# Delta-rule attention: chunks of 8 tokens solved in two halves of 4, with masked key products that carry the errors on

## What is computed

```
def step(S, t):
    q_t, k_t, v_t, a_t, b_t = t
    y = einsum('bhvk,bhk->bhv', S, k_t)
    err = y - v_t
    S = a_t[..., None] * S - (b_t[..., None] * err)[..., None] * k_t[:, :, None, :]
    o = einsum('bhvk,bhk->bhv', S, q_t)
    return (S, o)
```

## Time and profile before

| | us |
|---|---|
| median of 3 runs | 2726.8 |
| traced execution | 2720.65 |
| its span | 2718.9 |
| delta attention, its setup to its last block | about 986 to 2400 of the span |
| one part of 32 tokens, from the first base to the first state addition | 78.8 |

### The profile page before, as it was taken

How to read it: one execution, slowest core, us unless ns; L and a number is a source line. 1 busy time by engine, 2 the same in 40 slices (tenths; PEclk the granted TensorE clock), 3 DMA queues, 4 the chain that set the end, 5 groups by cost and what they waited for, 6 DMA issues and landing times. The chain is left out here.

```text
span 2718.9 us, 42746 instructions
## 1 busy us (share of the span) xinstructions
PE 2081.5 (77%) x15844; PEld 1636.3 (60%) x15856; DVE 1592.5 (59%) x3191; ACT 1141.1 (42%) x2723; POOL 1175.9 (43%) x996
## 2 busy tenths in 40 slices
PE   7597449978988968657896578955689656768798
PEld 5364126656566857646776567755568655546586
DVE  2223732246664339668776787766778677546533
ACT  3112311136464428434464344743446434325433
POOL 0222022210004535968339683386733877300254
PEclk9698769979998979767797677976779757789899
DMA  8422022210007023422223222232222332020340
GB/s 282 125 24 53 0 69 43 24 38 2 22 2 231 0 34 109 126 95 94 86 74 125 96 94 86 74 119 101 94 77 80 111 114 93 32 56 2 93 138 15
DMA packets 137426, 212.96 MB, mean 78 GB/s; under 512 B 61184, under 2 KB 113680, under 8 KB 132112
## 3 DMA queue, kind: packets, MB, share of 16 engines
q1 hardware_dynamic: 129072, 200.11, 23.1%
q0 software_dynamic: 8160, 10.26, 2.4%
HBM read 187.97 MB, written 22.37 MB: 77 GB/s over the span
## 5 line engine op out<-in xcount | busy, mean ns | idle before, releaser
L2088 PE MATMUL PS<-ident,XT 128*128 128x128 f32 x512 | 112.8, 402 | 258.2 <-DVE XT L2460 245.5
L2402 DVE SCALAR_TENSOR_TENSOR XT<-M_delta,CW_delta,XT 128x256 f32<-128x256 f32 x576 | 249.9, 495 | 70.2 <-ACT M_delta L2271 40.6
L2088 PEld LDWEIGHTS PS<-ident,XT 128*128 128x128 f32 x512 | 90.4, 208 | 277.6 <-DVE XT L2460 132.7
L2037 PE MATMUL PS<-XP_delta,X 128*128 128x268 f32 (+1 forms) x1024 | 241.6, 388 | 5.5 <-DMA X<-in_L_attn_b_heads 5.5
L2037 PEld LDWEIGHTS PS<-XP_delta,X 128*128 128x128 f32 x1024 | 192.7, 189 | 55.7 <-issue 11.4
L1541 PE MATMUL PS<-XP_rffn,UW_rffn 128*128 128x512 f32 x816 | 194.6, 395 | 5.5 <-POOL UW_rffn L1495 4.6
L1976 POOL TENSOR_TENSOR DD_delta<-DD_delta,A_delta 128x64 f32<-128x64 f32 (+6 forms) x224 | 169.9, 759 | 39.2 <-ACT A_delta L2359 19.5
L1541 PEld LDWEIGHTS PS<-XP_rffn,UW_rffn 128*128 128x128 f32 x816 | 155.5, 191 | 39.5 <-issue 6.8
L1273 ACT ACTIVATE PR_attn<-PS,NM_attn 128x256 f32<-128x256 f32 (+1 forms) x384 | 130.7, 448 | 103.6 <-DVE NM_attn L1343 103.6
L1495 POOL TENSOR_TENSOR UW_rffn<-W_rffn,UW_rffn 128x512 fp32r<-128x512 f32 x34 | 44.1, 1298 | 296.0 <-ACT UW_rffn L1602 296.0
L561 POOL DMA_INDIRECT sums<-XS_moe,token_moe x46 | 71.7, 1559 | 221.0 <-ACT XS_moe L661 205.8
(11 more groups left out here) (414 smaller groups left out, 5068.6 us busy)
## 6 DMA issues: line engine op xcount, KB each, us to landing
M_delta<-gram_delta SPq DMA_DIRECT2D x32, 2304.0 KB, 8.7
X<-in_L_attn_b_heads SPq DMA_DIRECT2D x64, 512.0 KB, 3.4
EW<-in_L_ffn_w SPq DMA_DIRECT2D x24, 512.0 KB, 10.0
CB_rffn<-routes_rffn SPq DMA_DIRECT2D x20, 512.0 KB, 22.4
XN<-in_L_attn_b_outs SPq DMA_DIRECT2D x16, 512.0 KB, 3.6
F_delta<-in_L_attn_b_outs SPq DMA_DIRECT2D x4, 2048.0 KB, 8.5
W_rffn<-in_L_ffn_tiles SPq DMA_DIRECT2D x4, 1536.0 KB, 11.6
slots<-pad SPq DMA_DIRECT2D x2, 2967.0 KB, 14.7
```

The source lines that it names most:

```text
L2037: last = nc.tensor.matmul(PS[:, 1 + i, 0:B * (WIN - halo)], WH[:, r, i, k, :], XP[:, k, :, n * BT + halo:n * BT + WIN], start=(k == 0), st ...
L2088: last = nc.tensor.transpose(PS[:, 6 + r % 2, i * P:(i + 1) * P], W[:, B * h:B * (h + 1), :], core.ident[:])
L2402: nc.vector.scalar_tensor_tensor(TMP[:, r, i], RAW[:, r, i, :, tau:tau + BT], CW[:, i, h, tau:tau + 1], TMP[:, r, i], ALU.mult, ALU.add).t ...
```

## The change

- A chunk is solved in two halves of 4 tokens (`HC`). The pairs kept in `M` and `DD` fall from 36 to 20 per lane, all within a half. `solve` runs three pairs of instructions per half.
- What the first half's errors do to the second half is made by TensorE: VectorE writes the errors times decays (`WH4`, `wh_d`), TensorE transposes them (2 transposes, `ht_mm`), ScalarE copies them (`NH4`, `nh_d`), TensorE multiplies them with `GH` (8 products, `res_mm`), and VectorE applies decays (`carry`) and adds.
- `GH` and `GN` are masked key products, made once per part (`key_products`): 32 and 96 products of separately copied keys (`keys_apart`), copied out by ScalarE and multiplied on GpSimd by beta and a mask that keeps a lane's own rows (`own_lanes`). For that, beta is also computed in rows in the stage's setup, turned, and moved through DRAM (`BETAC`, `BETAH`).
- What earlier chunks do to the next one is made by hops: 4 transposes of one chunk's `WNS`, one copy on ScalarE, 16 products with `GN` (`hop`). Chunk `jj` has `jj + 1` hops. The sum is accumulated in PSUM over a part of zeros (`ZB`).
- `W` is turned for the state update only once per part of 32 tokens; its first three chunks are copied there by ScalarE (12 copies).
- ScalarE's lanes per chunk are 10, 18, 18, 18. `DC` has two buffers. The answer copy comes after the next step in ScalarE's order (`answer`). The small tiles of `Norm` become slices of one scratch tile, the same size of work everywhere.

The core of the diff. GpSimd's products of decays, in `prepare`:

```diff
-                for t in range(C - 1, 0, -1):
-                    last = nc.gpsimd.tensor_tensor(DD[:, :, tri(t - 1) + 1:tri(t)], DD[:, :, tri(t):tri(t + 1)],
-                                                   step(t).broadcast_to([P, BH, C - t]), ALU.mult)
-                    if t > 1:
+                for u in range(HC - 1, 0, -1):
+                    last = nc.gpsimd.tensor_tensor(dd[:, :, :, tri(u - 1) + 1:tri(u)], dd[:, :, :, tri(u):tri(u + 1)],
+                                                   av[:, :, :, u:u + 1].broadcast_to([P, BH, 2, HC - u]), ALU.mult)
+                    if u > 1:
...
+                c.then(nc.gpsimd.tensor_tensor(dr[:, :, 1:], dd[:, :, 1, 0:HC], av[:, :, 1, 0:1].broadcast_to([P, BH, HC]), ALU.mult))
+                c.then(nc.gpsimd.tensor_tensor(dc[:, :, 1:HC + 1], dd[:, :, 0, 0:HC], av[:, :, 0, 0:1].broadcast_to([P, BH, HC]), ALU.mult))
+                c.then(nc.gpsimd.tensor_tensor(dc[:, :, HC + 1:], dr[:, :, 1:], dc[:, :, HC:HC + 1].broadcast_to([P, BH, HC]), ALU.mult))
```

TensorE, the order within a chunk, and a hop:

```diff
+                        first_half(n, ci)
+                        if jj == 0:
...
+                        elif jj < NI - 1:
+                            pe.wait_ge(res_d, z["res_d"] + ci + 1)
+                            for k in range(4):
+                                nc.tensor.matmul(PS[:, 1 + k, 0:4 * QU], ZB[:, 0:P], ZB[:], start=True, stop=False)
+                            for x in range(jj):
+                                hop(n, o, jj, x)
                         pe.wait_ge(w_d, z["w_d"] + ci + 1)
-                        if jj:
+                        if jj + 1 < NI:
+                            hop(n, o, jj, jj)
+                        else:
                             pe.wait_ge(wdec_d, z["wdec_d"] + rests(o, jj))
-                        for r in range(NR):
-                            turn(n, ci, r)
-                        if jj + 1 < NI:
-                            rest(n, o, jj + 1)
+                            for r in range(NR):
+                                turn(n, o, r)
...
+            def hop(n, o, jj, s):
...
+                if s < jj:
+                    pe.wait_ge(wdec_d, z["wdec_d"] + rests(o, jj))
+                for i in range(4):
+                    last = nc.tensor.transpose(PS[:, 6, i * P:(i + 1) * P], WNS[:, s, i * P:(i + 1) * P], core.ident[:])
+                last.then_inc(nw_mm, 1)
...
+                pe.wait_ge(nw_d, x)
+                for i in range(4):
+                    for k in range(4):
+                        rows, at = slice(OC * k, OC * (k + 1)), slice(i * QU, (i + 1) * QU)
+                        last = nc.tensor.matmul(PS[:, 1 + k, at], NEW[rows, i], GN[rows, BLOCKS.index((s, jj + 1)), at], start=jj == 0,
+                                                stop=jj == 0 or (s == jj and i == 3))
+                if s == jj:
+                    last.then_inc(rest_mm, 1)
```

ScalarE, the order within a chunk:

```diff
+                        if jj == NI - 1:
+                            act.wait_ge(wdec_d, z["wdec_d"] + rests(o, jj - 1))
+                            for x in range(NI - 1):
+                                for i in range(4):
+                                    last = nc.scalar.copy(W[:, :, x * C:(x + 1) * C].rearrange("p (k i b) t -> p i k b t", i=4, b=B)[:, i],
+                                                          WNS[:, x, i * P:(i + 1) * P].rearrange("p (k b t) -> p k b t", k=4, b=B))
+                            last.then_inc(nat_d, 1)
+                        act.wait_ge(ht_mm, z["ht_mm"] + ci + 1)
+                        nc.scalar.copy(NH4, PS[:, 7, 0:BH * HC]).then_inc(nh_d, 1)
...
+                        elif jj < NI - 1:
+                            for x in range(jj):
+                                hop(n, o, jj, x)
                         for lane in range(cuts[jj], cuts[jj + 1]):
                             last = nc.scalar.activation(S[:, lane, :], S[:, lane, :], ACT.Copy, scale=AO[:, lane:lane + 1])
-                        if jj == NI - 1:
+                        if jj < NI - 1:
+                            hop(n, o, jj, jj)
+                        else:
```

VectorE, `chunk`, between the two halves and behind the second:

```diff
+                solve(k, 0)
                 dve.wait_ge(ds_d, z["ds_d"] + o + 1)
...
+                base(o, jj, r, 1, FQ).then_inc(base_d, 1)
+                dve.wait_ge(wh_d, z["wh_d"] + ci + 1)
+                c.then(nc.vector.tensor_tensor(near, near, HJ[:, :, jj, 1:2].broadcast_to([P, BH, HC]), ALU.mult))
+                dve.wait_ge(res_mm, z["res_mm"] + ci + 1)
+                c.then(carry(r, 0))
+                c.then(nc.vector.tensor_tensor(FK[:, :, HC:], FK[:, :, HC:], carried(0), ALU.add))
+                solve(k, 1)
...
+                carry(r, 1).then_inc(res_d, 1)
```

416 lines of the change are left out of this document (302 added, 114 removed).

## The result

The changed kernel takes 2789.4 us (median of four runs, 2784.8 to 2790.6), the kernel before on the same chip 2725.0 (2723.1 to 2727.4): a ratio of 1.0233, 95% interval 1.0215 to 1.0251, or +64 us where +81 was forecast. (A block is 340 to 343 us long before, by its first bases at 1114.9, 1454.9, 1798.1 and 2141.3, and not about 320.) The page gives the span and busy times of the changed kernel; in the earlier trace rows GpSimd was busy for 1175.9 us, VectorE for 1592.5.

A forecast was written before the change was run, and what follows sets the result against it. GpSimd was taken to bound the chunks, VectorE 1.2 us behind. 4 x (3.7 + 11.2) + 16 + 5 = 81 us on 2720.65 gave 2801.7, and 2808 us with the median 6.2 higher; range 2725 to 2855.

The forecast's parts named there:

- GpSimd no longer bounds: Inner chunks: GpSimd drops from 21 to some 15.5 us and no longer bounds.
- The decay chain: A part's decay chain on GpSimd: four strided products of 512, up to 2.25 us each, 9 us, as much as before.
- W to late product: Behind `w_d`: late product after 11.25 us (second chunk), 14.9 (third), against VectorE's 6.9; stalls 4.3 and 8.0 us.
- First parts +3.7: Each block's first part of four chunks: 82.5 us against 78.8, +3.7.
- Second parts +11.2: Each block's second part, with gates on TensorE: 93.3 us at low clock, 80 at full, taken at 90, +11.2.
- Setup +16: Stage setup: beta in rows, turned and moved by DMA, all behind the old end: +16 us, between 10 and 22.
- States +5: States: seven more ScalarE copies, 1.2 us per block where no gap is: +5 us (0 to 10).
- A (clock): Rival: PE at full clock in the parts, shrinking hops, round trips and gates: +18, 2745 us; chance 0.16.
- B (VectorE ends each chunk): Rival: second and third chunks, late product within 6.9 us of `w_d`: faster, -41, 2686 us; chance 0.15.
- C (GpSimd dearer): Rival: GpSimd's three- and four-dimensional instructions cost 40% more than by elements: +48, 2856 us; chance 0.07.

The follow-up runs named there:

- its order mended: Changed kernel with GpSimd's decays within the next chunk issued ahead of its own lanes on the later key products: 2793.8 us, ratio 1.0256.
- The lanes alone: Changed kernel with ScalarE's state lanes behind the copy of the chunk's last hop instead of ahead of it: 2752.5 us, ratio 1.0119.
- The split: Changed kernel with the last third of the later key products behind the first half in a part's first chunk: 2806.6 us, ratio 1.0307.
- lanes and carries moved: Changed kernel with ScalarE's lanes behind the hop's copy and both VectorE carries ahead of the second half's solve: 2716.0 us, ratio 0.9984.

## Why the prediction was right, and which terms were off

*GpSimd no longer bounds.* Right. Its parts went from 75.0 busy us to 64.5, and inside a first part only the second chunk's base waits for it (2.4 us; 1.1 in three of four with its order mended). From one query product to the next (1508.74 to 1523.71) it needs 15.0 us in an inner chunk, 15.5 forecast. The forecast's own terms do not give its "5.7 us less", though: seven products of decays summed to 5.3 us before, so 3.0 + 2.25 less, and 1.0 more for the start decays, make 4.2. GpSimd also loses less to VectorE's key product now, but no run separates that.

*The decay chain.* The row's stride price held and not the rule of the Trainium skill cited there: the forecast had up to 2.25 us for each of four products, the trace has 2.1 to 2.2 (two of the first three, and the fourth):

```profile
1470.06 4.31 POOL L2018 TENSOR_TENSOR X<-X,A_delta 128x512 f32<-128x512 f32 x2
1474.44 2.11 POOL L2019 TENSOR_TENSOR HJ_delta<-X,A_delta 128x512 f32<-128x512 f32 x1
```

*W to late product.* Right in place, chain and length. From the base to the end of W 10.35 us were forecast, 10.4 measured (with a round trip twice as long the forecast's terms give 12.65, not its 12). From base to base 21.6 and 25.25 us were forecast, 21.4 and 25.2 measured. The stall in the third chunk came as forecast (8.15 for 8.0), that in the second at half (2.2 for 4.3), because one term of VectorE's own work was undersized: the key product took 3.60 us, not 1.6, in that place. The sum did not notice, since the stall only shrank by as much. That the chain is what costs is shown by the two edits that shorten it: together they take back .0249 of the time, all of the .0233 lost, although the setup's 15 us remain. The lanes alone, of which the forecast says "nothing hides them", were under half of it (.0114 of the .0249): 3.1 of their 5.35 us ran beside a hop's products and transposes on TensorE. The forecast's sum already has them so, beside the first hop; only its sentence does not.

*First parts +3.7.* Measured +5.1: the last chunk 16.1 to 16.5 instead of 15.65, and the first 19.5 to 22.1 instead of 20, with TensorE's key products issued in pieces with gaps of 1.3 and 2.0 us. The split shows that VectorE's wait there is not what costs; what sets the second base is GpSimd's order behind these products.

*Second parts +11.2.* Measured +11.1, and that is in part luck. The forecast's chunks (22, 23.6, 27.3, 20.4) sum to 93.3 at the low clock, and it took 90 for a clock in between without saying where that helps. Measured are 24.0, 22.2, 26.85 and 17.5: the first is 2 us too short in the forecast, the last 3 us too long. There the granted clock was 0.75, the four gates took 4.8 us and not 5.9, and the twelve copies behind them 0.21 us each and not 0.28.

*Setup +16.* From the end of beta (1012.9) to the first head weight pass 15.7 us, before 0.7: +15.0, of the forecast's 15.6. The products take 6.2 (4.9 forecast) and start 1.0 ahead of beta's end; sigmoids 1.3, turn 1.1, write 2.2, six issues 3.5 (2.4 forecast), landing 2.3.

*States +5.* Wrong, and the one term with the wrong sign: the forecast had ScalarE's seven copies lengthen the states, and the stretches between parts came out 10 us shorter. The heads' stretches took 141.1, 146.2 and 143.4 us before and 140.2, 140.2 and 140.9 after; in the other twelve profiled executions, all with the changed states, they take 139.3 to 142.0. So the copies' 1.2 us a block do not show, and two stretches of the one execution before were long. In the 146.2 the last of 128 small products was issued 4.4 us late:

```profile
1792.78 0.24 PE L2046 MATMUL PS<-KQ_delta 128*32 128x64 f32 x1 [4.38 <-issue]
```

In the 143.4 the granted clock was 0.92 where the 141.1 had 0.95, and TensorE was busy for 132.4 us in place of 129.4. Both look like chance of that execution; no second profile of the kernel before is there to show it.

*The rivals.* A (clock): the parts were granted 0.54 to 0.55 and 0.66, close to the 0.52 and 0.66 that the forecast took. With the waits shorter and the same products it is a little higher: 0.55 to 0.58 and 0.72 with lanes and carries moved. B (VectorE ends each chunk) needed the late product within 6.9 us of W; it took 10.8. With lanes and carries moved, B's mechanism came true at the third chunk's base, which no longer waits, but after 19.1 us and not 17.3, with a key product of 3.7 in them; the last chunk's base still waits 2.9 in first parts. C (GpSimd dearer): its packed products cost what elements said (1280 elements 2.9 us).

## What to carry to other kernels

When a result starts to travel through a second and third engine before its owner may go on, list what each of these engines has queued in front of it: here the small scalings on ScalarE held nobody up in the kernel before, where the bases waited for GpSimd, and 18 of them stood in the chain after. Release the far part of such a chain as early as its data are there, before the owner's own next work. And take a wait away only where the next wait is not for somebody else: removing the longest one of a first chunk made the kernel slower, because GpSimd was later than it.

## What the hardware showed

- **VectorE's product of two SBUF tiles and a GpSimd product exclude each other.** The key product (1264 elements) takes 1.47 or 1.48 us when GpSimd is idle at its start. At 1524.37 it finds GpSimd in its query product and ends at 1527.97, 1.33 us after GpSimd ended at 1526.64 (first line; the second is a key product with GpSimd idle):

```profile
1523.71 2.93 POOL L2092 TENSOR_TENSOR M_delta<-M_delta,DD_delta 128x1280 f32<-128x1280 f32 x1
...
1545.77 1.48 DVE L2658 TENSOR_TENSOR M_delta<-M_delta,DD_delta 128x1264 f32<-128x1264 f32 x1
```

  At 1484.32 it is the same: GpSimd's subtraction ends at 1485.50, the key product 1.34 us later. All 17 of the 32 key products that start while GpSimd works end 1.33 or 1.34 us after that GpSimd instruction; the other 15 take 1.47 or 1.48. The key product waits whole, it does not slow down. The Trainium skill says so too (SBUF — State Buffer, Who interferes with whom: an exclusive lock on the port pair shared by the two); the trace agrees.
- **GpSimd over a stride of four costs 4.1 ns an element**, 2.11 us for 512 with a result and both operands strided, against 2.1 to 2.5 ns packed (1.05 to 1.28 us for 512).
- **Small matmuls are issued in pieces.** The 192 matmul records of the later key products, 16 ns apart where they flow, come with gaps for which nothing in the profile is to blame:

```profile
1487.33 2.04 PE L2215 MATMUL PS<-KQ_delta,XT 128*32 128x64 f32 x128 [1.34 <-issue]
1491.36 1.17 PE L2215 MATMUL PS<-KQ_delta,XT 128*32 128x64 f32 x38 [2.00 <-issue]
```

  Their places vary from block to block.
- **The same code takes up to 10 us more where the granted clock is lower.** Turns, update and states of the second half take 42.8 us at 0.76 in the second block (the row of 1571.50 above) and 36.9 at 0.95 in the third, with VectorE busy for the same 15.8 us and TensorE for 36.6 and 30.0:

```profile
1929.05:1965.92 36.87, 30.02 (x513) 28.40 (x514) 15.79 (x13) 13.51 (x32) 9.93 (x12) 0.95 0.11 38
```

  Over the thirteen profiled executions with this code it is 36.8 to 37.0 us wherever the clock was 0.95 and 45.6 to 47.0 where it was 0.70 or 0.71. An effect of a few us can't be read from a single execution unless these stretches are taken out.
